# Folding Wv and Wo of six local-attention layers into one product per head, in a kernel on one core

## The chip, the core and the metric

The kernel runs on one core of a Trainium2 chip. The core has five engines, each with its own instruction stream: TensorE (PE; its weight loads are shown as PEld), VectorE (DVE), ScalarE (ACT), GpSimd (POOL) and SyncE (SP), which here only issues DMA copies. They synchronise by semaphores. Matmuls write to PSUM, eight banks of 512 fp32 columns by 128 partitions; the rest lives in SBUF. The metric is the device time of one execution in microseconds, as the median of several runs.

## The reference

x has 8 batch rows of 512 tokens by 128. An adaLN-modulated block applies a causal attention (16 heads of 8), then six local layers. One local layer is:

```python
def attn_layer(x, Wqkv, qs, ksc, Wo):        # Wqkv 128 x 3072, Wo 1024 x 128
    q, k, v = jnp.split(x @ Wqkv, 3, -1)     # 16 heads of 64
    q, k = l2norm(q) * qs, l2norm(k) * ksc   # per head
    ...                                      # rotary with scale on q and k
    out = local_attention(q, k, v)           # windows of 32, each sees itself and the one before
    return out.reshape(b, n, 1024) @ Wo
def ffn_layer(x, g, bln, W1, b1, W2, b2):    # layernorm, 128 -> 2 x 341, a * gelu(gate), -> 128
for i in range(6):
    x = attn_layer(shift_tokens(x), Wqkv[i], ...) + x
    x = ffn_layer(shift_tokens(x), ...) + x
```

`shift_tokens` takes the upper 64 dimensions from the token before. All is fp32.

## The kernel before

It has three parts, one after the other: the first attention (`modulated_attention`), the six local layers (`local_stack`), and a last residual.

**The local layers.** The work is cut into units, one batch row in one layer: 48 units, each of four tiles of 128 tokens. Each engine's program is a loop over units with the four tiles written out; the index d of a job says to which unit it belongs (0 this one, -1 the one before). The jobs of TensorE in one tile step stand in `jobs_of`, in the order in which TensorE runs them, each with its PSUM banks: the projections q, k and v (six fp32r matmuls each, of an input split in high and low parts), the transposes tq and tk of the tile before, ot (transposes of the attention's output o) of the tile three back, sim (the scores, 32 small products of 32 rows), pt (the transposes of the softmax weights), a feed job (m1 and m2 are the layernorm's mean and variance, y the second feed-forward product), z (Wo, eight products) and o (weights by values, 32 products), and in tile 1 the three hidden pieces h. `slot_free` makes TensorE wait until the earlier jobs in the same banks are taken out: so the table of banks decides which engine can hold up which job.

The other engines go through the same tiles in fixed orders. ScalarE squares q and k, copies qT, k_bd, v_tok, exponentiates the shifted scores in SBUF (`s`), copies oT and probT, makes the reciprocal norms by Ln and Exp, and does the layernorm's and gelu's functions. VectorE sums the squares, multiplies q and k by the cosine and sine tables (`rotate`), adds the mask, takes the maximum, sums the weights, divides o by the sum (L792), adds z and y to x. GpSimd adds the two halves of the rotation, applies the norms and subtracts the maximum.

The values go through SP: `spread_v` copies v_tok into v_bd, a layout with the windows of two heads side by side, block-diagonal with zeros, in eight copies a tile, and two more (the carried rows) from the tile before. v_tok and v_bd have two buffers, by the tile's parity. A value in `ready["o"]` two higher than the number of o jobs done lets SP fill a buffer once o of the tile two back is done. SP also loads the weights of the next layer (L337, in the last unit, before the last tile's spreading), the rotary tables, Wo and the feed-forward weights.

**The first attention** runs in 16 steps (heads) per batch row. Small jobs (`M_JOBS`: step, part, kind, distance in batches, group) use two banks in turn, so each waits for the one two places back. Beside it, one layer's Wqkv per batch row is split into high and low parts for the local layers: SP loads a third (L1052), GpSimd splits it (L1516, L1518), SP stores it (L1056).

## Time and profile before

| | |
|---|---|
| median of three runs | 3995.38 us (3992.62 to 4001.01) |
| the profiled execution | 4002.27 us, span 4000.5 us |
| mean granted TensorE clock | 0.985 |
| busy: PE / DVE / ACT / POOL | 93% / 79% / 64% / 70% |
| moved by DMA | 267.01 MB |

Times are in us from the start of the span unless marked ns. A clock of 1.00 is the upper of TensorE's two levels, 2.4 GHz. Matmuls overlap in the pipe and their ends are modelled, so how long one kind of job occupies TensorE is read from the start of the job to the start of the next. A wait shown in brackets is idle time just before an instruction, with the engine and line that ended it; "issue" means nothing that the profile shows.

### The profile page before, as it was taken

What the parts mean: (1) busy time and instruction counts of PE and PEld (TensorE: products, weight loads), DVE (VectorE), ACT (ScalarE), POOL (GpSimd) and SP (SyncE); (2) the same over time, 40 slices, a digit from 0 to 9 for tenths busy, and PEclk for the clock granted to TensorE, in tenths of its full rate; (3) what the DMA queues carried; (4) which work ended last, traced back from release to release, by engine and by line L of the source; (5) the groups of instructions that cost most, each with busy time, mean ns of one, the idle gap of its engine ahead of it and who ended that gap; (6) DMA issues with size and microseconds to landing.
All of it is one profiled execution on the core that took longest, in us unless ns stands there. A gap on an engine that the chain in (4) does not pass through costs nothing. (4 is left out here: it accounts for less than half of the span.)

```text
span 4000.5 us, 109740 instructions
## 1 busy us (share of the span) xinstructions
PE 3733.8 (93%) x42284; PEld 2927.6 (73%) x42284; DVE 3151.4 (79%) x4328; ACT 2570.7 (64%) x3589; POOL 2781.7 (70%) x2249
## 2 busy tenths in 40 slices
PE   6998897799999999999999999999999999999996
PEld 4766675677777777777777777777777777777774
DVE  4666664888888888888888888888888888888884
ACT  3555554566666666666666666666666767676763
POOL 2554552777777777777777777777777777777772
PEclk9999998999999999999999999999999999999998
DMA  1122110322223222232222232222322223222222
GB/s 42 59 74 73 66 68 13 100 66 60 62 63 100 66 58 64 55 103 63 68 53 66 82 79 64 61 61 62 102 66 62 60 60 99 62 70 54 68 54 62
DMA packets 157178, 267.01 MB, mean 67 GB/s; under 512 B 32062, under 2 KB 51644, under 8 KB 152380
## 3 DMA queue, kind: packets, MB, share of 16 engines
q1 hardware_dynamic: 157116, 266.19, 24.7%
q8 instruction: 38, 0.62, 0.1%
q14 instruction: 24, 0.20, 0.0%
HBM read 44.81 MB, written 26.21 MB: 18 GB/s over the span
## 5 line engine op out<-in xcount | busy, mean ns | idle before, releaser
L826 POOL TENSOR_TENSOR st_qk_rot<-st_qk_rot,st_qk_sq 128x1024 f32<-128x1024 f32 x384 | 920.5, 2402 | 692.7 <-DVE st_qk_sq L728 692.7
L455 PE MATMUL st_ps<-st_wqkv,st_xs 128*128 128x512 f32 x3456 | 949.6, 410 | 25.8 <-issue 18.3
L455 PEld LDWEIGHTS st_ps<-st_wqkv,st_xs 128*128 128x128 f32 x3456 | 608.2, 189 | 194.6 <-issue 75.2
L846 POOL TENSOR_TENSOR st_qk_rot<-st_qk_rot,st_rn 128x1024 f32<-128x1024 f32 x384 | 723.1, 1904 | 15.0
L710 DVE TENSOR_REDUCE st_nt<-st_qk_sq 128x16 f32<-128x1024 f32 x384 | 466.2, 1214 | 234.6 <-ACT st_qk_sq L573 233.2
L728 DVE TENSOR_TENSOR st_qk_sq<-st_ps,st_rot 128x512 f32<-128x512 f32 x768 | 490.1, 678 | 0.0
L714 DVE TENSOR_TENSOR st_qk_rot<-st_ps,st_rot 128x1024 f32<-128x1024 f32 x384 | 466.1, 1214 | 9.8 <-PE st_ps L472 9.8
L472 PE MATMUL st_ps<-consts_sb,st_qk_rot 128*128 128x128 f32 x3072 | 402.2, 274 | 27.9 <-DVE st_hid L802 14.9
L571 ACT ACTIVATE st_qk_sq<-st_ps 128x512 f32<-128x512 f32 x192 | 115.0, 599 | 486.3 <-PE st_ps L455 485.8
L472 PEld LDWEIGHTS st_ps<-consts_sb,st_qk_rot 128*128 128x128 f32 x3072 | 355.8, 141 | 94.1 <-DVE st_hid L802 34.7
L465 PEld LDWEIGHTS st_ps<-st_oT,st_wo 128*128 128x128 f32 x3072 | 368.8, 192 | 69.5 <-issue 67.7
L1458 DVE TENSOR_REDUCE at_nmx<-at_s 128x1 f32<-128x512 f32 (+3 forms) x512 | 236.9, 486 | 209.3 <-PE at_s L1103 208.5
L608 ACT ACTIVATE st_k_bd<-st_ps 64x1024 f32<-64x1024 f32 x384 | 389.5, 1014 | 3.1 <-PE st_ps L472 0.8
L485 PE MATMUL st_ps<-st_k_bd,st_qT 128*32 128x128 f32 x12288 | 375.2, 274 | 3.0 <-ACT st_k_bd L608 3.0
L465 PE MATMUL st_ps<-st_oT,st_wo 128*128 128x128 f32 x3072 | 376.2, 276 | 0.5 <-ACT st_oT L632 0.3
L497 PE MATMUL st_ps<-st_v_bd,st_probT 128*32 128x128 f32 x12288 | 375.2, 274 | 1.3 <-ACT st_probT L640 1.3
L874 POOL TENSOR_TENSOR st_s<-st_s,st_mx 128x1024 f32<-128x1024 f32 x192 | 366.0, 1906 | 6.1 <-DVE st_mx L753 6.1
L1279 ACT ACTIVATE at_probT<-at_t 128x512 f32<-128x512 f32 (+1 forms) x384 | 201.3, 526 | 255.8 <-PE at_t L1122 248.1
L485 PEld LDWEIGHTS st_ps<-st_k_bd,st_qT 128*32 128x32 f32 x12288 | 326.4, 110 | 35.6 <-ACT st_k_bd L608 20.5
L497 PEld LDWEIGHTS st_ps<-st_v_bd,st_probT 128*32 128x32 f32 x12288 | 323.7, 110 | 24.5 <-issue 1.5
L522 PE MATMUL st_ps<-st_xc,st_w 128*128 128x512 f32 (+1 forms) x576 | 261.8, 604 | 52.6 <-DVE xT_sb L784 43.2
L1542 POOL TENSOR_TENSOR at_qs<-at_q,consts_sb 128x512 fp32r<-128x512 f32 x128 | 135.3, 1074 | 216.8 <-DVE at_q L1409 200.0
(144 smaller groups left out, 6944.8 us busy)
## 6 DMA issues: line engine op xcount, KB each, us to landing
st_v_bd<-st_v_tok SPq DMA_DIRECT2D x1152, 128.0 KB, 2.4
st_v_bd<-st_v_tok SPq DMA_DIRECT2D x672, 64.0 KB, 2.1
wqkv_parts<-at_w_parts SPq DMA_DIRECT2D x18, 1024.0 KB, 4.6
st_wqkv<-wqkv_parts SPq DMA_DIRECT2D x18, 1024.0 KB, 7.0
at_w_raw<-in_wqkv SPq DMA_DIRECT2D x18, 512.0 KB, 5.1
rotary_tables<-at_rot SPq DMA_DIRECT2D x6, 512.0 KB, 3.4
st_rot<-rotary_tables SPq DMA_DIRECT2D x24, 128.0 KB, 2.4
st_wo<-in_wo SPq DMA_DIRECT2D x6, 512.0 KB, 4.4
```

The source lines that it names most:

```text
L455: last = pe.matmul(out[:, c * 512:(c + 1) * 512], xs[:, x_part, t * P:(t + 1) * P], rhs, start=(n == 0), stop=(n == len(PASSES) - 1))
L465: last = pe.matmul(out[:, 0:P], wo[:, c, :], oT[:, c * P:(c + 1) * P], start=(c == 0), stop=(c == IC - 1))
L472: last = pe.transpose(out[:, c * P:(c + 1) * P], src[:, c * P:(c + 1) * P], ident)
L485: last = pe.matmul(out[g * WIN:(g + 1) * WIN, c * P:(c + 1) * P], qT[:, par, c * P + g * WIN:c * P + (g + 1) * WIN], k_bd[:, c, :, key:key ...
L497: last = pe.matmul(out[g * WIN:(g + 1) * WIN, c * P:(c + 1) * P], probT[:, c * P + g * WIN:c * P + (g + 1) * WIN], v_bd[:, par, g, :, c * ...
L608: last = act.activation(k_bd[rows, :, a, WIN + t1 * P:WIN + (t1 + 1) * P], src[rows, :, :], ACT.Copy)
L710: dve.tensor_reduce(nt[:, 2 + par, heads], qk_sq[:, cols].rearrange("p (h d) -> p h d", d=DH), AX.X, ALU.add).then_inc(ss_sum, 1)
L714: dve.tensor_tensor(qk_rot[:, cols].rearrange("p (h d) -> p h d", d=DH), slot_of("qk"[a], 0, t).rearrange("p (h d) -> p h d", d=DH), rot[: ...
L728: last = dve.tensor_tensor(dst[:, :, g, :], src[:, :, 1 - g, :], sines.unsqueeze(1).to_broadcast([P, HEADS, DH // 2]), ALU.mult)
L826: pool.tensor_tensor(qk_rot[:, cols], qk_rot[:, cols], qk_sq[:, cols], ALU.add).then_inc(rot_done[a], 1)
L846: pool.tensor_tensor(view, view, rn[:, par, heads_of(a)].unsqueeze(2).to_broadcast([P, HEADS, DH]), ALU.mult).then_inc(normed[a], 1)
L874: pool.tensor_tensor(scores, scores, mx[:, tt % 2, :].unsqueeze(2).to_broadcast([P, HEADS, 2 * WIN]), ALU.subtract).then_inc(shifted, 1)
```

## The change

**Folding.** For each head, v times Wo's rows of that head equals x times (Wv Wo) of that head, a 128 by 128 matrix. The changed kernel makes these sixteen matrices once a layer, in the first attention: new small jobs transpose Wv's third of Wqkv (`vt`, two jobs of four transposes), multiply by Wo's rows (`fold`, four jobs of four products, a contraction of 64), ScalarE writes the high part, VectorE the low part, and SP stores 2048 columns, v0 (first heads of the pairs) and v1 (second heads). GpSimd splits only q and k.

**Projection.** The local layers project q, k, v0 and v1: four groups of six matmuls instead of three. A value row has 2048 columns instead of 1024.

**Products.** v_win has for each window 128 rows (two heads by 64 keys) and 128 columns per pair of heads. The 32 products of a tile now add up over the eight pairs into one 128-column bank, z. No zeros are needed, and the 8 transposes of o and the 8 products with Wo are gone. z (tokens first) is copied to SBUF (`z_tok`), transposed once (`zt`), and added to x.

**Softmax.** ScalarE exponentiates into PSUM banks 4 and 5 (`ex`), VectorE sums the weights there, and divides them there while writing them to `s`; pt transposes weights that are already divided, one tile later than before.

**Carried rows.** The last window of a tile is copied to `v_held` as soon as v is there, and from there into the next tile's windows. The spreading waits for z of the tile two back.

```diff
-H_BANKS = ((0, 1), (6, 7), (2, 3))
+H_BANKS = ((6, 7), (0, 1), (4, 5))
+PROJ = ("q", "k", "v0", "v1")
...
-            feed = {3: [(("m1", -1, 0), (1,))], 0: [(("m2", -2, 0), (1,))], 1: [], 2: [(("y", -2, 0), (1,))]}[t]
+            feed = {3: [(("m1", -1, 0), (6,))], 0: [(("m2", -2, 0), (6,))], 1: [], 2: [(("y", -2, 0), (6,))]}[t]
             hidden = [(("h", -2, j), H_BANKS[j]) for j in range(HC)] if t == 1 else []
-            return [tile("q", 0, 0, 1), tile("tq", 1, 2, 3), tile("k", 0, 4, 5), tile("tk", 1, 6, 7),
-                    tile("v", 0, 2, 3), tile("ot", 3, 0, 1), tile("sim", 1, 6, 7), tile("pt", 2, 2, 3), *feed,
-                    tile("z", 3, 0), tile("o", 2, 4, 5), *hidden]
+            return [tile("q", 0, 0, 1), tile("tq", 1, 2, 3), tile("k", 0, 4, 5), tile("ex", 2, 4, 5), tile("tk", 1, 6, 7),
+                    tile("v0", 0, 2, 3), tile("pt", 3, 0, 1), tile("sim", 1, 6, 7), tile("v1", 0, 0, 1), tile("z", 3, 2),
+                    *feed, *hidden, tile("zt", 3, 7)]
...
+                    for kind in ("v0", "v1"):
+                        sp.wait_ge(taken[kind], tiles_done(u, 0, t))
+                    if t < TILES - 1:
+                        d, carried = ((-1, 3), (-1, 2), (0, 1))[t]
+                        if alive(u, d):
+                            sp.sem_inc(filled, 1)
+                            sp.wait_ge(carry_in[carried % 2], carry_count(u, d, carried))
+                        for a in range(2):
+                            sp.dma_start(v_held[held_rows(t, a), :], v_tok[P - WIN:P, par, a, :]).then_inc(held_in[par], 16)
+                    sp.wait_ge(ready["z"], tiles_done(u, 0, t))
+                    if t:
+                        sp.sem_inc(filled, 1)
+                        sp.wait_ge(held_in[1 - par], held_count(u, 0, t - 1))
+                        for a in range(2):
+                            sp.dma_start(v_win[a * 2 * WIN:a * 2 * WIN + WIN, par, 0, :], v_held[held_rows(t - 1, a), :])\
+                              .then_inc(carry_in[par], 16)
                     for a in range(2):
                         rows = slice(a * 2 * WIN, (a + 1) * 2 * WIN)
-                        cols = slice(a * INNER // 2, (a + 1) * INNER // 2)
                         for g in range(1, WPT):
-                            sp.dma_start(v_bd[rows, par, g, a, :], v_tok[(g - 1) * WIN:(g + 1) * WIN, par, cols])\
-                              .then_inc(vbd_in[par], 16)
-                        sp.dma_start(v_bd[a * 2 * WIN + WIN:(a + 1) * 2 * WIN, par, 0, a, :], v_tok[0:WIN, par, cols])\
-                          .then_inc(vbd_in[par], 16)
+                            sp.dma_start(v_win[rows, par, g, :], v_tok[(g - 1) * WIN:(g + 1) * WIN, par, a, :])\
+                              .then_inc(win_in[par], 16)
+                        sp.dma_start(v_win[a * 2 * WIN + WIN:(a + 1) * 2 * WIN, par, 0, :], v_tok[0:WIN, par, a, :])\
+                          .then_inc(win_in[par], 16)
...
+                        if what == "wqkv" and t >= TILES - 2:
+                            for kind in (("q", "k"), ("v0", "v1"))[t - (TILES - 2)]:
+                                sp.wait_ge(ready[kind], tiles_done(u, 0, TILES - 1))
                                 load_wqkv(layer + 1, kind)
...
+                            elif kind == "zt":
+                                pe.wait_ge(taken["z"], tiles_done(u, d, index))
+                                last = pe.transpose(out[:, 0:P], z_tok[:, :], ident)
...
-                                            out[g * WIN:(g + 1) * WIN, c * P:(c + 1) * P],
+                                            out[g * WIN:(g + 1) * WIN, 0:P],
                                             probT[:, c * P + g * WIN:c * P + (g + 1) * WIN],
-                                            v_bd[:, par, g, :, c * DH:(c + 1) * DH], start=True, stop=True)
-                            elif kind == "ot":
-                                pe.wait_ge(taken["o"], tiles_done(u, d, index))
-                                for c in range(IC):
-                                    last = pe.transpose(out[:, c * P:(c + 1) * P], o[:, c * P:(c + 1) * P], ident)
+                                            v_win[:, par, g, c * P:(c + 1) * P], start=(c == 0), stop=(c == IC - 1))
...
+                        def copy_v(a):
+                            act.wait_ge(ready[f"v{a}"], n)
+                            if not (start and n < 3):
+                                act.wait_ge(win_in[t % 2], spread_count(u, d2, t2))
+                                if t2 < TILES - 1:
+                                    act.wait_ge(held_in[t2 % 2], held_count(u, d2, t2))
+                            act.activation(v_tok[:, t % 2, a, :], slot_of(f"v{a}", 0, t), ACT.Copy).then_inc(taken[f"v{a}"], 1)
...
+                            slot_free(act, u, STARTS[t] + EX_AT)
+                            act.activation(slot_of("ex", d2, t2), s[:, t2 % 2, :], ACT.Exp).then_inc(ready["ex"], 1)
...
+                            act.activation(z_tok[:, :], slot_of("z", d3, t3)[:, 0:P], ACT.Copy).then_inc(taken["z"], 1)
...
+                            dve.wait_ge(ready["ex"], n - 2)
+                            weights = slot_of("ex", d2, t2).rearrange("p (h k) -> p h k", h=HEADS)
+                            dve.tensor_reduce(den[:, t2 % 2, 0, :], weights, AX.X, ALU.add).then_inc(den_ready, 1)
                             dve.wait_ge(den_ready, 2 * (n - 2) - 1)
                             dve.reciprocal(den[:, t2 % 2, 1, :], den[:, t2 % 2, 0, :]).then_inc(den_ready, 1)
+                            dve.wait_ge(den_ready, 2 * (n - 2))
+                            dve.tensor_tensor(s[:, t2 % 2, :].rearrange("p (h k) -> p h k", h=HEADS), weights,
+                                              den[:, t2 % 2, 1, :].unsqueeze(2).to_broadcast([P, HEADS, 2 * WIN]),
+                                              ALU.mult).then_inc(taken["ex"], 1)
...
-SPLIT_STEPS = (2, 6, 14)
+SPLIT_STEPS = (5, 11)
...
-                  (7, 0, "round", -1, 3), (8, 0, "den", -1, 3), (8, 1, "mt", 0, 1), (9, 0, "rd", -1, 3),
+                  (7, 0, "round", -1, 3), (7, 1, "fold", 0, 0), (7, 1, "fold", 0, 1), (8, 0, "den", -1, 3), (8, 1, "mt", 0, 1), (9, 0, "rd", -1, 3),
...
+                def split_weights(layer):
+                    load_raw(layer, 2)
+                    sp.dma_start(wo_l[:, :, :], w["wo"][bass.ds(layer, 1), :, :].rearrange("l (c p) n -> p (l c) n", p=P))\
+                      .then_inc(fold_in, 16)
+                    sp.wait_ge(taken["vt"], layer * 2 + 4)
+                    sp.sem_inc(filled, 1)
+                    for a in range(2):
+                        load_raw(layer, a)
+                        sp.wait_ge(split_done, layer * 2 + (a + 1))
+                        store_parts(layer, a, w_parts[:, :, :])
+                def store_folded(layer):
+                    for a in range(2):
+                        sp.wait_ge(taken["fold"], layer * 4 + (2 * a + 6))
+                        store_parts(layer, 2 + a, fold_parts[:, a, :, :])
...
+                    elif kind == "vt":
+                        pe.wait_ge(raw_in, (b - 1) * 48 + 16)
+                        for i in range(TILES):
+                            at = (TILES * g + i) * P
+                            last = pe.transpose(out[:, i * P:(i + 1) * P], w_raw[:, at:at + P], ident)
+                    elif kind == "fold":
+                        rows, half = slice(g // 2 * DH, (g // 2 + 1) * DH), g % 2
+                        pe.wait_ge(taken["vt"], count(b, 0, 2, half))
+                        pe.wait_ge(fold_in, (b - 1) * 16 + 16)
+                        for i in range(TILES):
+                            c = TILES * half + i
+                            last = pe.matmul(out[:, i * P:(i + 1) * P], wvT[rows, c, :], wo_l[rows, c, :],
+                                             start=True, stop=True)
...
+                    elif kind == "vt":
+                        act.wait_ge(ready["vt"], count(b, d, 2, g))
+                        if g == 0:
+                            act.wait_ge(taken["fold"], count(b, -1, 4, 3))
+                        act.activation(wvT[:, TILES * g:TILES * (g + 1), :].rearrange("p c n -> p (c n)"), src[:, :], ACT.Copy)\
+                           .then_inc(taken["vt"], 1)
+                    elif kind == "fold":
+                        act.wait_ge(ready["fold"], count(b, d, 4, g))
+                        if g == 0:
+                            act.wait_ge(parts_out, (b - 1) * 64 + 16)
+                        act.activation(fold_parts[:, g // 2, 0, g % 2 * 512:g % 2 * 512 + 512], src[:, :], ACT.Copy)\
+                           .then_inc(fold_high, 1)
```

Three places in the order of instructions:

TensorE, one tile step before the unit's end, from the job after v on (st_o: attention output, st_s: weights, st_oT: its transpose), before:

```order
L505 MATMUL st_ps<-consts_sb,st_o 128x128 [waits st_o_taken,st_rot_read_q,st_squared_q]
L505 MATMUL st_ps<-consts_sb,st_o 128x128 x7
L485 MATMUL st_ps<-st_k_bd,st_qT 32x128 [waits st_tq_taken,st_tk_taken]
L485 MATMUL st_ps<-st_k_bd,st_qT 32x128 x31
L477 MATMUL st_ps<-consts_sb,st_s 128x128 [waits st_exp_ready,st_v_taken]
L477 MATMUL st_ps<-consts_sb,st_s 128x128 x7
L509 ISA [waits st_z_taken,st_ot_taken]
L509 MATMUL st_ps<-xT_sb,consts_sb 128x512
L465 MATMUL st_ps<-st_oT,st_wo 128x128 [waits st_wo_in,st_ot_taken]
L465 MATMUL st_ps<-st_oT,st_wo 128x128 x7
L494 REGISTER_ALU [waits st_pt_taken,st_vbd_in1,st_rot_read_k,st_squared_k]
L497 MATMUL st_ps<-st_v_bd,st_probT 32x128 [waits st_carry_in1]
```

and after, from the job after v0 on:

```order
L480 MATMUL st_ps<-consts_sb,st_s 128x128 [waits st_ex_taken,st_rot_read_q,st_squared_q]
L480 MATMUL st_ps<-consts_sb,st_s 128x128 x7
L488 MATMUL st_ps<-st_k_bd,st_qT 32x128 [waits st_tq_taken,st_tk_taken]
L488 MATMUL st_ps<-st_k_bd,st_qT 32x128 x31
L460 MATMUL st_ps<-st_wqkv,st_xs 128x512 [waits st_pt_taken]
L460 MATMUL st_ps<-st_wqkv,st_xs 128x512 x5
L495 REGISTER_ALU [waits st_pt_taken,st_v0_taken]
L500 MATMUL st_ps<-st_v_win,st_probT 32x128 [waits st_win_in0]
L500 MATMUL st_ps<-st_v_win,st_probT 32x128 x31
L507 ISA [waits st_zt_taken,st_sim_taken]
L507 MATMUL st_ps<-xT_sb,consts_sb 128x512
L469 MATMUL st_ps<-consts_sb,st_z_tok 128x128 [waits st_z_taken,st_sim_taken]
```

The transposes of o (L505) and the sixteen Wo instructions (L465) are gone; a projection (L460) stands between sim and the products, the products wait for v0 and the windows, and the mean product (L507) and one transpose (L469) come last.

VectorE, the last part of that tile, after the rotation, before:

```order
L749 TENSOR_TENSOR st_s<-st_ps,consts_sb 128x1024 [waits st_pt_ready,st_sim_ready]
L753 TENSOR_REDUCE st_mx<-st_s 128x16 [waits st_sim_taken]
L757 TENSOR_REDUCE st_den<-st_s 128x16 [waits st_exp_ready]
L760 RECIPROCAL st_den<-st_den 128x16 [waits st_den_ready]
L766 ISA [waits st_h_ready,st_m1_ready]
L766 TENSOR_TENSOR st_xc<-xT_sb,st_ps 128x512
L784 ISA [waits st_z_ready]
L784 TENSOR_TENSOR xT_sb<-st_ps,xT_sb 64x128
L784 ISA
L784 TENSOR_TENSOR xT_sb<-st_ps,xT_sb 64x128
L792 TENSOR_TENSOR st_o<-st_ps,st_den 128x1024 [waits st_ot_ready,st_den_ready,st_o_ready]
```

and after:

```order
L761 TENSOR_TENSOR st_s<-st_ps,consts_sb 128x1024 [waits st_pt_ready,st_sim_ready]
L768 TENSOR_REDUCE st_den<-st_ps 128x16 [waits st_ex_ready]
L770 RECIPROCAL st_den<-st_den 128x16 [waits st_den_ready]
L772 TENSOR_TENSOR st_s<-st_ps,st_den 128x1024 [waits st_den_ready]
L783 ISA [waits st_h_ready,st_m1_ready]
L783 TENSOR_TENSOR st_xc<-xT_sb,st_ps 128x512
L788 TENSOR_REDUCE st_mx<-st_s 128x16 [waits st_sim_taken]
L799 ISA [waits st_zt_ready]
L799 TENSOR_TENSOR xT_sb<-st_ps,xT_sb 64x128
L799 ISA
L799 TENSOR_TENSOR xT_sb<-st_ps,xT_sb 64x128
```

The division has moved from the end (o) to behind the reciprocal, where it works on the weights; the maximum has moved behind it and behind the layernorm's subtraction; z now waits for zt.

SP, in the last unit of a layer, around the loads of the next layer's weights, before:

```order
L360 ISA [waits st_rot_read_k]
L360 DMA st_rot<-rotary_tables 128x256
L397 REGISTER_ALU
L337 ISA [waits st_q_ready]
L337 DMA st_wqkv<-wqkv_parts 128x2048
L337 ISA [waits st_k_ready]
L337 DMA st_wqkv<-wqkv_parts 128x2048
L337 ISA [waits st_v_ready]
L337 DMA st_wqkv<-wqkv_parts 128x2048
L371 DMA st_v_bd<-st_v_tok 32x512 [waits st_o_ready,st_v_taken]
L371 DMA st_v_bd<-st_v_tok 32x512
L377 DMA st_v_bd<-st_v_tok 64x512 x3
```

and after, from the rows set aside for tile 2 on:

```order
L382 DMA st_v_held<-st_v_tok 32x1024
L387 REGISTER_ALU [waits st_z_ready]
L389 DMA st_v_win<-st_v_held 32x1024 [waits st_held_in1]
L389 DMA st_v_win<-st_v_held 32x1024
L394 DMA st_v_win<-st_v_tok 64x1024 x3
L396 DMA st_v_win<-st_v_tok 32x1024
L394 DMA st_v_win<-st_v_tok 64x1024 x3
L396 DMA st_v_win<-st_v_tok 32x1024
L367 ISA [waits st_rot_read_k]
L367 DMA st_rot<-rotary_tables 128x256
L349 ISA [waits st_v0_ready]
L349 DMA st_wqkv<-wqkv_parts 128x2048
```

Before, the three loads stood ahead of the last tile's copies. Now q's and k's stand ahead of the third tile's copies, v0's and v1's behind them, and those copies wait for z.

## Rows read from the trace of the kernel before

**Rows 1.** Windows by stage: length, busy per engine (count), PEclk, DMA share, GB/s.
```profile
300.00:450.00 150.00, 134.25 (x945) 103.00 (x935) 98.53 (x200) 86.20 (x167) 80.09 (x72) 0.98 0.22 77
2000.00:3000.00 1000.00, 971.03 (x11907) 770.24 (x11910) 843.72 (x1074) 685.02 (x897) 762.14 (x609) 1.00 0.27 70
```

**Rows 2.** st_wqkv's loads, then TensorE's timeline: start, us, what, count [idle before].
```profile
L337 SPq MOVE st_wqkv<-wqkv_parts x12: 29/29/38, 1755.8 to 3369.4; - x12
...
263.79 2.36 PE L1148 MATMUL at_m<-at_probT,at_v_pad 128*32 128x512 f32 x32
...
2007.06 1.06 PE L505 MATMUL st_ps<-consts_sb,st_o 128*128 128x128 f32 x8 [0.37 <-issue]
...
2017.34 1.66 PE L455 MATMUL st_ps<-st_wqkv,st_xs 128*128 128x512 f32 x6
2018.83 1.04 PE L472 MATMUL st_ps<-consts_sb,st_qk_rot 128*128 128x128 f32 x8
...
2023.37 1.04 PE L505 MATMUL st_ps<-consts_sb,st_o 128*128 128x128 f32 x8
2024.36 1.95 PE L485 MATMUL st_ps<-st_k_bd,st_qT 128*32 128x128 f32 x64
...
2028.33 1.95 PE L465 MATMUL st_ps<-st_oT,st_wo 128*128 128x128 f32 x16
2030.20 1.95 PE L497 MATMUL st_ps<-st_v_bd,st_probT 128*32 128x128 f32 x64
...
2061.92 5.41 PE L522 MATMUL st_ps<-st_xc,st_w 128*128 128x512 f32 x12 [0.94 <-DVE xT_sb L784]
...
2069.10 1.10 PE L472 MATMUL st_ps<-consts_sb,st_qk_rot 128*128 128x128 f32 x8 [0.33 <-DVE st_hid L802]
```

**Rows 3.** VectorE: waits of 800 to 3900; its timeline; the division's group.
```profile
DVE st_nt L710 <- ACT st_qk_sq L573: 227.5, 184, 1.7
DVE st_hid L802 <- ACT st_hid L670: 179.6, 93, 3.3
...
2034.79 1.22 DVE L710 TENSOR_REDUCE st_nt<-st_qk_sq 128x16 f32<-128x1024 f32 x1 [1.34 <-ACT st_qk_sq L573]
...
2041.96 0.41 DVE L686 TENSOR_TENSOR st_xs<-xT_sb,st_xs 128x256 fp32r<-128x256 f32 x1
...
L792 DVE TENSOR_TENSOR st_o<-st_ps,st_den 128x1024 f32<-128x1024 f32 x36 | 44.1, 1225 | 9.5 <-PE st_ps L497 8.6
```

**Rows 4.** ScalarE's timeline: rstd, the next square, the table after gelu.
```profile
2045.04 0.63 ACT L656 ACTIVATE st_rstd<-st_rstd 128x512 f32<-128x512 f32 x1
2048.13 0.60 ACT L571 ACTIVATE st_qk_sq<-st_ps 128x512 f32<-128x512 f32 x1 [2.46 <-PE st_ps L455]
...
2068.18 1.28 ACT L672 ACT_TABLE_LOAD   x1
```

**Rows 5.** SP's timeline of one burst; windows in bursts; st_wqkv's loads to landing.
```profile
2032.27 1.17 SPq L371 DMA_DIRECT2D st_v_bd<-st_v_tok  x2
...
2037.95 0.59 SPq L379 DMA_DIRECT2D st_v_bd<-st_v_tok  x1
...
2034.00:2036.00 2.00, 2.00 (x14) 1.68 (x13) 1.21 (x2) 1.53 (x2) 2.00 (x2) 1.00 0.71 164
1221.00:1223.00 2.00, 2.00 (x13) 1.52 (x13) 1.97 (x3) 1.18 (x2) 2.00 (x2) 1.00 1.02 430
...
DMA to landing us min/median/max: 4.9/7.0/10.2
```

**Rows 6.** TensorE's timeline at the start of the local layers.
```profile
722.95 1.94 PE L472 MATMUL st_ps<-consts_sb,st_qk_rot 128*128 128x128 f32 x8 [7.71 <-POOL st_qk_rot L846]
```

**Rows 7.** First attention: SP's stores of x1; the v job's group, 150 to 600.
```profile
400.01 0.33 SPq L1040 DMA_DIRECT2D x_dims_first<-at_x  x1
...
478.24 0.33 SPq L1040 DMA_DIRECT2D x_dims_first<-at_x  x1
...
L1173 PE MATMUL at_m<-at_wv,at_hT 128*128 128x128 f32 x42 | 6.2, 287 | 5.0 <-DVE at_aT L1428 5.0
```

266 lines of the change are left out of this document (124 added, 142 removed), and 3 rows, old and new, of the table M_JOBS.

## The prediction

> **What bounds the kernel now.** I read the windows by stage first, then TensorE's order of time over one unit, then the waits of VectorE, and last the copies. In the first attention TensorE is busy for 134 of 150 us. In the local layers it is busy for 971 of 1000 us, with VectorE at 844, ScalarE at 685, GpSimd at 762 and a granted clock of 1.00 [rows 1]. So TensorE sets the local stage, and VectorE is the engine behind it.
>
> The period of the local stage comes from the weight loads: from the group at 1755.8 to the last of the group three layers later, 3369.4, it is 1613.6 us less about 1 within a group, for 24 units (a unit is one batch row in one layer, four tiles): 67.2 us a unit [rows 2]. There are 48 units. In start-to-start times, a projection of six matmuls takes 1.49 (2017.34 to 2018.83), the eight transposes of o 0.99 (2023.37 to 2024.36), the sixteen instructions of Wo 1.87 (2028.33 to 2030.20). Three waits are seen in a unit: 0.37 before the transposes of o, 0.94 before the hidden layer, 0.33 before a query transpose [rows 2].
>
> VectorE's own work is 0.844 x 67.2 = 56.7 us a unit. It idles for ScalarE's squares (227.5 us over 184 tiles, 1.24 each) and for gelu (179.6 us over 46 units, 3.9 each) [rows 3]: it is ready early and waits for what TensorE feeds it.
>
> **Local layers, TensorE.** Removed per unit: 4 x (0.99 + 1.87) = 11.4 us, and the three waits, 1.64, since each hangs on a buffer that the new table of banks gives to another job or that is no longer made. Added: a fourth projection group, 4 x 1.49 = 5.96, and one transpose per tile, 4 x 0.15 = 0.6 (0.99 over eight, with something for the turn). The products with the weights stay 32 a tile with 128 columns; only where they add up changes. v_pad's products of the first attention already add up in strips of 32: 1280 columns in 2.36 us, 1.84 ns each, while o's 1024 take 1.95 us, 1.90 ns each [rows 2]. So I take no change (bounds 0 and +0.5 a tile). The work is then 67.2 - 11.4 - 1.6 + 6.0 + 0.6 = 60.8.
>
> New waits, found by setting the other engines' rows against that order:
> (a) The variance product now stands right before zt and the next q, with no z and o behind it (3.8 us). ScalarE makes rstd of it, until 2045.67 in the trace, and squares q at 2048.13 [rows 4]. With q 3.7 us sooner that square could start at 2044.4, so it comes about 1.2 late. VectorE starts late with it, and pt, whose banks are those of q, waits about 0.5.
> (b) After gelu ScalarE loads its table again, 1.28 [rows 4], so VectorE starts the next tile some 0.8 late: about 0.5 before pt.
> (c) VectorE has 7.2 us of rotation before the scores (2034.79 to 2041.96 [rows 3]), then mask, sum, division and maximum, some 1.2 each, and the reciprocal and z, 0.8 together: 12.8 us, in a tile for which TensorE needs 13.6: 60.8 less some 9.9 of small products (22 instructions like the twelve of the hidden layer, 5.41 [rows 2]) over four, and one small product. With the hidden layer it is 17.7. It fits with little to spare; I put 0.4 a unit for the places where it doesn't.
> Sum 1.4: a unit of 62.2, 5.0 less. These rates hold from about 745, when the pipeline has filled, to 3915: 3170 / 67.2 = 47 units, **-235 us**.
>
> VectorE's and ScalarE's work stays: the division reads the same 1024 columns from PSUM as the one over o did (1225 ns [rows 3]), the copy of v1 takes the place of oT's, z_tok adds an eighth of such a copy and its start, some 0.3 a tile. The sum over weights moves its source from SBUF to PSUM. A reduction of 1024 from SBUF takes 1.22 us and the product from PSUM 1225 ns [rows 3]: I take 0, bounds -0.05 and +0.1 a tile. By the Trainium skill (VectorE: DVE Perf Modes, the section on the TRN2 errata) an instruction with a source in PSUM has a fixed cost 62 cycles above one with a source in SBUF, some 65 ns. That would be 12 us of VectorE over 192 tiles, inside its spare time. The rows show no such difference at this size.
>
> **The copies.** Each tile issues ten copies for its windows as before, and two more for the rows set aside. Ten issues take 6.3 us (2032.27 to 2038.54 [rows 5]). A row of a copy has 4 KB instead of 2 KB, so a burst has 2.1 MB instead of 1.05. With 2 KB rows a burst used 0.71 of the queues at 164 GB/s, which is 230 at full share; with 8 KB rows the weights moved 430 GB/s at 1.02 [rows 5]. In time per row this is 142 and 305 ns on each of 16 queues, and between them some 196 ns at 4 KB: 330 GB/s, or 6.4 us a burst, as long as its issue. A weight load of 1.05 MB lands 4.9 us after its issue at the least [rows 5], of which 2.4 is transfer, so the last copy lands about 6.3 + 2.5 + 0.2 = 9.0 after z. The new waits hang on this: v_tok of a tile is written again in the tile after next, but its windows are only free after z of the tile two back, which comes one tile later than o did. From the end of z to ScalarE's copy of v0 there are at least 1 us of small products, then q, tq, k, tk, v0, pt and the copy of probT: about 9.3 us in the tightest tile. It just fits: 0, bounds 0 and +1 us in two tiles of a unit.
>
> **Layer boundaries.** SP is in order. The loads of v0 and v1 now stand behind the third tile's windows, which wait for the z of the tile two back; before, all three loads went out ahead of the last tile's windows. From the end of that z: ten issues 6.3, a table 0.6, then v0's load, which lands 4.9 later [rows 5]: 11.8. TensorE wants v0 after m1 0.9, zt 0.15, and q, tq, k, tk, which took 4.54 (2017.34 to 2023.37, less v's 1.49 [rows 2]): 5.6. It stands for 6.2 us. After 7.71 us of standing, eight transposes took 1.94 instead of 1.04 [rows 6], and I allow the same once more for what follows: 8 us at each of five boundaries, **+40** (bounds 0 and 60).
>
> **First attention.** Batches follow each other at 78.2 us (400.01 to 478.24 [rows 7]). Six of them get two jobs of four transposes (0.5 each) and four folding jobs, each four products like the v job (6.2 us over 5.25 jobs and some overlap [rows 7]: 0.95): 4.8 us of TensorE. They share two banks with all small jobs, each job waits for the one two back, and a folding job is released only after ScalarE's copy and VectorE's subtraction a step later. I add 1.5 a batch: 6.3 x 6 = **+38** (bounds: 14, if half the work sinks into the 8 us a batch in which TensorE waits now [rows 1], and 65, if each of the six jobs makes a wait of 1). GpSimd loses a third of the splitting, which nobody waits for.
>
> At the start a fourth load stands before the small ones: +2.4, less a little for the shorter clearing, **+2**. The tail I leave as it is.
>
> Sum: -235 + 40 + 38 + 2 = -155 on the profiled execution's 4002.3: 3847. The median of the runs is 3995.4, 0.2% lower, so **3840**.
>
> **Rivals.**
> *VectorE takes over.* It has 56.7 us of work a unit, and its idle time may hang on the order and not on TensorE's pace. If the 1.24 per tile before the squares stays, and a third of gelu's 3.9, it is 63.0, and 64 with delays that push each other: 3.2 x 47 = 150 gained, 80 paid, 3925. For it: 12.8 in 13.6 is little room, and z of the tile now comes last on both engines. Against: the banks let VectorE lag. 0.2.
> *The additions are free.* The loads come in time, and the folding sinks into present waits: -235 + 14 + 2, 3775. SP's order speaks against it. 0.1.
> *The windows' copies set the pace: slower.* If a burst moves no more than the 164 GB/s seen, 2.1 MB takes 12.8 us and lands 15.1 after z; the copy of v0 (1.0) and z (1.9), whose bank was v0's, close the loop: 18.0 a tile, 72 a unit, 4.8 x 47 + 80 = +306, 4300. It decides for slower from 65.5 a unit on, a landing 13.5 after z. Against it: the share was 0.71, not 1. The Trainium skill (DMA: Bandwidth & Descriptors, "Why small descriptors are slow") says that copies within SBUF don't pay for small rows, and that the fabric limits them at 435 GB/s. The 230 at full share with 2 KB rows does not agree with that, the 430 with 8 KB rows does; by it a burst would take 4.8 us. 0.05.
> *Adding up in one bank costs what the fold saves*, 1.2 us a tile: about 3995. v_pad's row speaks against it. 0.03.
>
> **Numbers.** The forecast has 0.62: 3840. The range is 3765 to 3925, from free additions to VectorE's case. Against the 0.2% that a measurement tells from no change: faster 0.92, the same 0.03, slower 0.05.
>
> **What the profile will show.** A unit of 62 us with TensorE near 60 and VectorE over 90%; no wait before the hidden layer, short ones before pt; bursts of ten copies in 6 us, the last landing 9 us after z; five gaps of 6 us before v0; batches of 84 us in the first attention; some 510 MB moved. I am wrong if a unit takes over 64, if ScalarE's copy of v0 waits for copies in each tile, or if batches grow by more than 11 us.

## The result, and the profile after

| | before | after |
|---|---|---|
| median, us (4 runs each, side by side) | 3997.92 (3992.62 to 4001.01) | 4059.08 (4052.26 to 4062.88) |
| ratio | 1 | 1.0152, 95% interval 1.0133 to 1.0172 |
| span of the profiled execution | 4000.5 | 4059.3 |
| loads for the local layers issued at | 696.8 | 746.3 |
| period of a unit | 67.2 | 65.7 |
| a unit across a layer boundary, less that | 0 | 13.1 (10.5 to 16.4) |
| moved by DMA | 267.01 MB | 512.39 MB |

The change makes the kernel 1.5% slower; the forecast was 3840. A unit's period is read from one first gelu to the next. After, in ScalarE's timeline (start, us, engine, line; an idle time before in brackets):

```profile
2055.63 1.26 ACT L679 ACTIVATE st_hid<-st_ps,st_b 128x512 f32<-128x512 f32 x2
...
2121.32 1.26 ACT L679 ACTIVATE st_hid<-st_ps,st_b 128x512 f32<-128x512 f32 x2
```

65.7 us, where 62.2 was forecast. TensorE no longer fills the stage, and no other engine does; the window that answers to [rows 1]:

```profile
2000.00:3000.00 1000.00, 911.49 (x10899) 674.31 (x10899) 855.77 (x1069) 683.37 (x949) 765.35 (x608) 0.98 0.65 142
```

The waits of 900 to 3900 (engine, tile, line, releaser: us, times, longest) say what stands between them:

```profile
ACT st_v_tok L598 <- DMA st_v_win<-st_v_tok: 227.3, 129, 3.0
...
DVE st_den L768 <- ACT st_ps L633: 145.3, 129, 2.1
...
PE st_ps L480 <- issue: 92.3, 173, 1.0
...
PE st_ps L500 <- ACT st_v_tok L598: 79.9, 85, 1.7
...
PE st_ps L460 <- DMA st_wqkv<-wqkv_parts: 56.3, 8, 11.1
```

ScalarE's copy of v0 waits for the window copies in 129 tiles: three of the four of a unit. Behind it stand its own exponential, for which VectorE waits as often (129 times), and z, whose bank is v0's. The loop can be followed in one tile. TensorE, then SP's queue, then ScalarE:

```profile
2034.47 1.95 PE L500 MATMUL st_ps<-st_v_win,st_probT 128*32 128x128 f32 x64 [0.95 <-ACT st_v_tok L598]
...
2044.62 1.06 PE L480 MATMUL st_ps<-consts_sb,st_s 128*128 128x128 f32 x8 [0.95 <-issue]
...
2050.08 1.95 PE L500 MATMUL st_ps<-st_v_win,st_probT 128*32 128x128 f32 x64 [0.93 <-ACT st_v_tok L598]
```

```profile
2036.69 1.17 SPq L389 DMA_DIRECT2D st_v_win<-st_v_held  x2
...
2040.97 2.60 SPq L394 DMA_DIRECT2D st_v_win<-st_v_tok  x3
2043.61 0.99 SPq L396 DMA_DIRECT2D st_v_win<-st_v_tok  x1
```

```profile
2048.92 1.02 ACT L598 ACTIVATE st_v_tok<-st_ps 128x1024 f32<-128x1024 f32 x1 [2.18 <-DMA st_v_win<-st_v_tok]
```

z ends at 2036.4, the ten copies are issued from 2036.69 to 2044.6 (8 us, not 6.3), the last has landed at 2048.9, 12.5 after z; then the copy of v0, and the next z at 2050.08: 15.6 us round. The next round has the hidden layer in it and lasts to 2069.13, 19.1 us; there the loop has time. Over the whole stage the medians from one z to the next are 15.4, 15.6, 19.1 and 15.7 us. The queues are full in such a burst (the share is the last but one number, GB/s the last); over the four windows of 2008 to 2016 the rate is 197 to 260, on average 221:

```profile
2008.00:2010.00 2.00, 2.00 (x14) 1.70 (x12) 1.94 (x5) 0.94 (x2) 2.00 (x2) 1.00 1.04 197
```

At a layer boundary TensorE stands for v0's weights. SP's queue, and TensorE:

```profile
1279.63 0.94 SPq L349 DMA_DIRECT2D st_wqkv<-wqkv_parts  x2
```

```profile
1289.30 2.90 PE L460 MATMUL st_ps<-st_wqkv,st_xs 128*128 128x512 f32 x6 [11.01 <-DMA st_wqkv<-wqkv_parts]
```

The load is issued behind ten window copies and a table and its data arrive 9.7 us later, behind theirs. From this projection's start to the next job's (1292.00) it is then 2.70 us instead of 1.49 [rows 2], at the lower clock level (granted 0.50 from 1289 to 1293). At three of the five boundaries TensorE had also waited for k's weights, 1.1 to 3.5 us. In the first attention, between the stores of x1 (78.2 us before [rows 7]) lie 89.6 us:

```profile
430.04 0.33 SPq L1060 DMA_DIRECT2D x_dims_first<-at_x  x1
519.61 0.33 SPq L1060 DMA_DIRECT2D x_dims_first<-at_x  x1
```

From the traces alone: 49.5 us in the first attention (746.3 against 696.8), 66 at the five boundaries, 5 in filling the pipeline (to the first gelu), 5 in the last two periods, less 1.47 (67.18 against 65.71) for each of the other 45 periods, 66. Sum about +59; the spans differ by 58.8.

### The profile page after: what moved, and what is told of

It reads as the page before. It is cut to its first block and busy times, and to the rows that moved or that the text cites. A ratio compares the mean times of both kernels' runs of the same rounds, so it can differ in the third digit from the quotient of the medians.

```text
span 4059.3 us, 104487 instructions
## 1 busy us (share of the span) xinstructions
PE 3598.6 (89%) x39260; PEld 2658.4 (65%) x39260; DVE 3208.4 (79%) x4352; ACT 2604.8 (64%) x3817; POOL 2756.6 (68%) x2238
## 2 busy tenths in 40 slices
DMA packets 172730, 512.39 MB, mean 126 GB/s; under 512 B 36862, under 2 KB 56444, under 8 KB 166396
## 5 line engine op out<-in xcount | busy, mean ns | idle before, releaser
L460 PE MATMUL st_ps<-st_wqkv,st_xs 128*128 128x512 f32 x4608 | 1273.3, 412 | 99.7 <-DMA st_wqkv<-wqkv_parts 56.3
L460 PEld LDWEIGHTS st_ps<-st_wqkv,st_xs 128*128 128x128 f32 x4608 | 815.7, 190 | 336.9 <-issue 194.0
L598 ACT ACTIVATE st_v_tok<-st_ps 128x1024 f32<-128x1024 f32 x384 | 389.9, 1015 | 248.5 <-DMA st_v_win<-st_v_tok 244.2
L500 PE MATMUL st_ps<-st_v_win,st_probT 128*32 128x128 f32 x12288 | 376.1, 274 | 90.1 <-ACT st_v_tok L598 86.7
L500 PEld LDWEIGHTS st_ps<-st_v_win,st_probT 128*32 128x32 f32 x12288 | 325.1, 110 | 165.0 <-issue 155.9
L883 POOL TENSOR_TENSOR st_s<-st_s,st_mx 128x1024 f32<-128x1024 f32 x192 | 374.3, 1949 | 48.7 <-DVE st_mx L788 48.7
L768 DVE TENSOR_REDUCE st_den<-st_ps 128x16 f32<-128x1024 f32 x192 | 235.0, 1224 | 162.6 <-ACT st_ps L633 160.5
L625 ACT ACTIVATE st_probT<-st_ps 128x1024 f32<-128x1024 f32 x192 | 196.9, 1025 | 231.2 <-PE st_ps L480 231.2
L480 PE MATMUL st_ps<-consts_sb,st_s 128*128 128x128 f32 x1536 | 208.9, 280 | 98.9 <-issue 97.7
```

The costliest lines, as they stand in the source:

```text
L460: last = pe.matmul(out[:, c * 512:(c + 1) * 512], xs[:, x_part, t * P:(t + 1) * P], wqkv[:, PROJ.index(kind), w_part, c * 512:(c + 1) * 51 ...
L500: last = pe.matmul(out[g * WIN:(g + 1) * WIN, 0:P], probT[:, c * P + g * WIN:c * P + (g + 1) * WIN], v_win[:, par, g, c * P:(c + 1) * P], ...
L598: act.activation(v_tok[:, t % 2, a, :], slot_of(f"v{a}", 0, t), ACT.Copy).then_inc(taken[f"v{a}"], 1)
L883: pool.tensor_tensor(scores, scores, mx[:, tt % 2, :].unsqueeze(2).to_broadcast([P, HEADS, 2 * WIN]), ALU.subtract).then_inc(shifted, 1)
```

## Experiments

Each kernel is the changed one with the edit shown; of an edit only the lines that matter stand here, some of them shortened, and the counts of the semaphores follow. Ratios are to the kernel before, run beside it, with 95% intervals; after it stands at 1.0152.

### 1. v0's copy waits for its own half of the windows only

```diff
-act.wait_ge(win_in[t % 2], spread_count(u, d2, t2))
+act.wait_ge(win_in[t % 2][a], spread_count(u, d2, t2))
```

Each half's copies have a semaphore of their own, and z waits for both.

> ScalarE's copy of v0 waits only for the window copies that read v0's half of v_tok (the first five of a burst's rows of it), and that of v1 for the others; the number and size of copies stay. Theory A (the handoff of v_tok through the window copies sets three of the four tiles of a unit: z, burst of 8.0 us, last landing 4.6 later, copy of v0 1.0, next z): v0's copy is released four issues earlier, 3.7 us, its waits of 1.1 to 2.2 us go, and a unit falls from 65.7 to 62.2 to 63.0 us; 45 units give -120 to -155 us: 3905 to 3940, ratio to the kernel before 0.977 to 0.986. Theory B (the waits for copies only show what another chain, ScalarE and VectorE around the exponential in PSUM, would take anyway): a unit stays within 0.7 of 65.7 and the time at 4030 to 4060, ratio 1.008 to 1.015. The five gaps at the layer boundaries stay in both.

Measured: 3958.47, ratio 0.9907 (0.9891 to 0.9924). A unit takes 63.6 us. ScalarE's wait for window copies is gone; the boundaries cost 12 to 17 as before, now 13.4. Nothing was made faster, the wait only leaves out the four window copies of the other half: theory A holds for 2.1 of the 3.5 us. It leaves 1.4 open, and the time came out 18 us above its range. The rounds from z to z are now 14.0, 15.1, 18.9 and 15.7 us (medians). So of the three waits of v0's copy two cost TensorE time, 1.4 and 0.5 us; the third, in the round of 15.7, which has the second feed-forward product in it, cost nothing.

### 2. All weight loads ahead of the third tile's burst

```diff
-if what == "wqkv" and t >= TILES - 2:
-    for kind in (("q", "k"), ("v0", "v1"))[t - (TILES - 2)]:
+if what == "wqkv" and t == TILES - 2:
+    for kind in PROJ:
```

> All four weight loads of the next layer are issued ahead of the third tile's burst; nothing else. Theory A: the wait for v0's weights of 9 to 11 us per boundary goes, but 4.2 MB now stand in front of one burst and hold the windows up, so some 5 us a boundary stay of the 13.5 that a boundary costs: 5 x 8.5 = -42 us, 4017, ratio 1.005 (1.001 to 1.009). Rival: the stall only moves to the windows behind the loads and the time stays at 4059, ratio 1.015.

Measured: 4033.09, ratio 1.0093 (1.0072 to 1.0114). A boundary costs 8.7 us instead of 13.1. TensorE no longer waits for weights there, but one tile later for z, since v0's copy waits for windows that are queued behind 4.2 MB. ScalarE and TensorE of this kernel:

```profile
1280.93 1.02 ACT L598 ACTIVATE st_v_tok<-st_ps 128x1024 f32<-128x1024 f32 x1 [9.26 <-DMA st_v_win<-st_v_tok]
```

```profile
1282.18 3.64 PE L500 MATMUL st_ps<-st_v_win,st_probT 128*32 128x128 f32 x64 [8.19 <-ACT st_v_tok L598]
```

### 3 and 4. No folding jobs; only the transposes of Wv

```diff
-(2, 1, "vt", 0, 0), (3, 1, "vt", 0, 1),
...
-(7, 1, "fold", 0, 0), (7, 1, "fold", 0, 1), (11, 1, "fold", 0, 2), (14, 1, "fold", 0, 3),
...
+store_parts(layer, 2 + a, w_parts[:, :, :])
```

> The first attention makes no folded weights: the six vt and fold jobs of a batch row are left out, Wv's third is loaded but not used, and the parts of q and k are stored a second time in the places of v0 and v1, so that SP moves the same bytes; the local layers do the same work on other numbers. If the jobs themselves (work and the waits of two banks) cost the 49.5 us by which the local layers start later than before: they start at 697 to 702 and the time falls by 45 to 50 us, to 4010 to 4015, ratio 1.003 to 1.005. Rival: a part of it comes from the splitting that moved to later steps and from SP's order: less than 30 us come back, ratio above 1.008.

> Of the folding jobs in the first attention only the two that transpose Wv's third stay; the four folding jobs of a batch row are left out, and q's and k's parts are stored in the places of v0 and v1. Leaving out all six gave back 54.7 us on the changed kernel's 4059.1. If a job's cost goes by its work on TensorE (two of four transposes 0.4 to 0.5 each, four of four products 1.1 each): the four are 44 to 50 of the 54.7, so 4010 to 4015, ratio 1.003 to 1.005. If each of the six costs alike through the two banks: 36 of it, 4023, ratio 1.0065.

Measured: 4004.41, ratio 1.0020 (1.0011 to 1.0030), and with vt 3999.79, ratio 1.0006 (0.9996 to 1.0015). The local layers' loads go out at 696.2 and at 690.9 (746.3 in the changed kernel). (The second run keeps the two vt jobs.) So leaving out the four folding jobs brings the loads 55 us forward, 9 a batch row (the total falls by 59), and leaving out the transposes too gives nothing more: more than either theory gave the four. The first run, without any of the six, has its loads 5 us later than the second; why is open. That in the second they go out 6 us before those of the kernel before (696.8) may come from GpSimd's shorter splitting, but the first run has that as well, and it was not tried alone.

### 5. Half the bytes

```diff
-sp.dma_start(v_win[rows, par, g, :], v_tok[(g - 1) * WIN:(g + 1) * WIN, par, a, :])
+sp.dma_start(v_win[rows, par, g, 0:512], v_tok[(g - 1) * WIN:(g + 1) * WIN, par, a, 0:512])
```

> Each window copy, the carried ones too, moves only the first 512 of its 1024 columns (2 KB rows, as in the kernel before), and the products read these twice: twelve copies a tile as in the changed kernel, half the bytes. Theory A: a burst is issued in 6.3 us and lands 2.4 us after its last issue, as before, so 8.9 after z instead of 12.4, and no copy of v0 waits: a unit of 62.2 to 62.8, the boundaries a little better, 3895 to 3930, ratio 0.974 to 0.983. Theory B: a unit stays at 65 to 65.7, ratio 1.008 to 1.015.

Measured: 3929.63, ratio 0.9831 (0.9815 to 0.9848). As many copies, half the bytes: SP's issue is back to 6.3 us, a copy lands after 2.4 us instead of 4.6, no copy of v0 waits, a unit takes 63.6 as in the first run, with the same four rounds, a boundary costs 8.0. It is the bytes that hold the handoff up, and 63.6 is the next limit.

### 6 and 7. Windows from DRAM, in copies of 64 and of 128 partitions

```diff
-sp.dma_start(v_win[rows, par, g, :], v_tok[(g - 1) * WIN:(g + 1) * WIN, par, a, :])
+sp.dma_start(v_win[rows, par, g, :], w_split[par, (g - 1) * WIN:(g + 1) * WIN, a * INNER:(a + 1) * INNER])
```

and in the second run, once for both halves:

```diff
+sp.dma_start(v_win[:, par, g, :], w_split[par, :, (g - 1) * 512:(g - 1) * 512 + INNER])
```

> The changed kernel with one thing else: the eight window copies of a tile, with the same 4 KB rows, the same destination and the same waits, read DRAM (the weights' scratch) and not v_tok, so the products use other numbers. It tells what made a burst of 2.1 MB take 9 us and more. Theory R (the length of the rows: a 4 KB row takes what it takes, near 300 ns a queue): the landing stays at 12.4 after z, a unit at 65 to 66, ratio 1.011 to 1.017. Theory S (the source in SBUF: the weights came from DRAM at 430 GB/s, copies within SBUF at some 225): a burst moves at over 350 GB/s, lands within 9.5 us after z, no copy of v0 waits, a unit of 63.6 as in the runs that released it, 3925 to 3960, ratio 0.982 to 0.991.

> As the run with the windows read from DRAM (4150 us, its bursts at 205 to 240 GB/s at full share), but each of the three whole windows of a tile comes in one copy of 128 partitions instead of two of 64; rows of 4 KB and bytes are the same. Theory P (what sets the rate is how many partitions a copy spans: 64 reach half of the SBUF's DMA ports, 128 all, as for the weights): the middle of a burst moves over 350 GB/s, the landing comes some 4 us earlier, a unit falls from 67.6 to 63.6 to 64.5, 3940 to 4000, ratio 0.986 to 1.001. Theory R (a 4 KB row costs 300 ns wherever it goes, and 8 KB rows cost no more): the rate stays near 215 GB/s and a unit at 66 or above, ratio above 1.02.

Measured: 4150.39, ratio 1.0390 (1.0373 to 1.0407), and 3942.43, ratio 0.9858 (0.9842 to 0.9874). Of the first run's two theories the one on the source fell: from DRAM a copy lands later (5.5 us against 4.6), the burst moves no faster, and v0's copy starts 13.2 us after z against 12.5. Theory R's range (a unit of 65 to 66) was missed as well: a unit takes 67.7. R still seemed nearer, until the second run, with rows of the same 4 KB, came to twice the rate in the middle of a burst, at full share. (It has five copies for eight, but the queues are full in both.) Its unit is 63.6; v0's copy starts 2.5 us earlier than with 64 partitions, where 4 were expected. The run with 64 partitions, then that with 128:

```profile
2016.00:2018.00 2.00, 1.92 (x10) 1.61 (x11) 1.99 (x4) 1.97 (x3) 1.05 (x2) 1.00 1.07 225
```

```profile
2004.00:2005.00 1.00, 1.00 (x5) 0.83 (x5) 1.00 (x2) 0.98 (x2) 1.00 (x1) 1.00 1.05 422
...
2024.00:2025.00 1.00, 1.00 (x7) 0.82 (x6) 1.00 (x2) 1.00 (x2) 0.00 (x0) 1.00 0.98 401
```

What sets the rate is how many partitions a copy spans: from DRAM 64 get 203 to 231 GB/s in the windows of a burst at full share, 128 get 401 and 422 in the middle of a burst, as the weights did [rows 5]. The Trainium skill says so (SBUF — State Buffer, "Door 1: The DMA port swizzle"): partitions 0 to 63 reach eight of the SBUF's sixteen DMA ports, for some 218 GB/s, all 128 reach sixteen, for 436. Both levels agree with these runs; the ports themselves no trace shows.

The traces' records of single packets have the same step. A packet of 4 KB took 320 ns (median of a burst) to 64 partitions, from SBUF as from DRAM, and 159 in the middle of a burst to 128. To 64 partitions one of 2 KB took 142 ns, to 128 one of 8 KB 309. So the length of the rows has little part in it here. Copies within SBUF that span 128 partitions were not tried.

### 8. The two halves in turn

```diff
-for a in range(2):
-    for g in range(1, WPT):
+for g in range(1, WPT):
+    for a in range(2):
```

> The changed kernel with the six copies of whole windows issued window by window, first heads' 64 partitions and then second heads', in turn, where they were issued all first heads' and then all second heads'. Bytes, rows and waits are the same. If copies to the two halves of the partitions overlap in the queues (theory P with some depth): full-share rate of 300 GB/s or more, landing 2 to 3 us earlier, a unit of 63.6, 3950 to 3965, ratio 0.989 to 0.992. If one copy after the other goes through all queues in step: 65.7 a unit, 4059, ratio 1.015.

Measured: 3992.43, ratio 0.9987 (0.9977 to 0.9996), from the order of issue alone. A unit takes 64.5, a boundary costs 10.7; the wait of v0's copy falls from 227.3 us to 167.0. It lies between the two expectations: two halves in turn overlap a little. Three of the kernel's windows:

```profile
2024.00:2025.00 1.00, 1.00 (x4) 0.20 (x2) 0.75 (x2) 0.60 (x2) 1.00 (x2) 1.00 1.04 320
2025.00:2026.00 1.00, 0.66 (x3) 0.36 (x3) 1.00 (x3) 0.52 (x1) 1.00 (x1) 1.00 1.01 234
2026.00:2027.00 1.00, 1.00 (x5) 0.82 (x5) 1.00 (x2) 0.98 (x2) 0.97 (x2) 1.00 1.08 246
```

The Trainium skill (SBUF — State Buffer, "Can I just issue two DMAs to hit both halves?") says no, with a gain of 6%. The size agrees: over nine such windows (2021 to 2030) the mean is 230 GB/s, against 221 over the four of 2008 to 2016 in the changed kernel. But the path hung on it: v0's copy starts 11.6 to 11.9 us after z where it was 12.2 to 12.5, and so 4% on each burst gave 1.6% of the kernel's time.

### 9. What holds a unit at 63.6

```diff
-dve.tensor_reduce(mx[:, t1 % 2, :], scores, AX.X, ALU.max)
+dve.tensor_reduce(mx[:, t1 % 2, :], scores[:, :, WIN:WIN + 8], AX.X, ALU.max)
```

Edit 1 is in it too.

> v0's copy waits only for its own half of the window copies, and VectorE takes the maximum over 8 of the 64 keys of a head (0.3 us for 1.2), 0.9 us less in each tile, which leaves most scores out of the maximum. It tells what holds a unit at 63.6 once the copies don't. If VectorE (890 of 1000 us busy there): a unit falls by 1 to 1.5 to 62.1 to 62.6, TensorE's own pace by the forecast, 3890 to 3912, ratio 0.973 to 0.979. If TensorE's work is simply longer than forecast: a unit stays at 63.6 and the ratio at 0.991.

Measured: 3922.6, ratio 0.9813 (0.9797 to 0.9830); a unit of 62.9. The four maxima of a unit take 276 ns instead of 1210: 3.7 us a unit taken from VectorE give 0.7. It is neither of the two cases, and the time is 11 us above the range of the first.

With edit 1 TensorE still waits 2.6 us in a unit: 0.95, 0.40 and 0.48 before pt, 0.34 before q's projection (for VectorE's product in the feed-forward layer) and 0.41 before a transpose (for GpSimd). Each of the three pt starts 0.1 us after VectorE's second read of q's bank ends. In the run with edit 1, VectorE, then TensorE:

```profile
2017.02 1.28 DVE L738 TENSOR_TENSOR st_qk_sq<-st_ps,st_rot 128x512 f32<-128x512 f32 x2
```

```profile
2018.40 1.06 PE L480 MATMUL st_ps<-consts_sb,st_s 128*128 128x128 f32 x8 [0.40 <-issue]
```

The wait of 0.95 comes where VectorE is busy without a break, and the lighter VectorE cuts it to 0.29. Those of 0.40 and 0.48 stay (0.41 and 0.46): there VectorE had stood idle for 0.66 and 0.32 before q's sum, in the run with edit 1 already, so its amount of work is not what they hang on. In both runs the period less the waits (2.6 and 1.9) is 61.0: TensorE's work, forecast at 60.8.

### 10 to 12. Edits together

> The two edits of the first runs together: v0's copy waits only for its own half of the window copies, and all four weight loads stand ahead of the third tile's burst. If the two costs are separate, the gains add up: 101 and 26 us, 3932, ratio 0.984 (0.981 to 0.987). With them the boundary's price is 8 us, since v0's own windows still stand behind 4.2 MB of weights. Rival: the earlier loads meet a burst that is now tighter and give back nothing: 3958, ratio 0.991.

> v0's copy waits only for its own half of the window copies; q's, k's and v0's loads stand ahead of the third tile's burst, v1's between its two halves. v0's windows then wait for 3.1 MB that had been asked for from 11 us before z on, so they land on time, and v1's load lands some 12 us after z where TensorE wants it 10 after: a boundary costs 3 us and not 13: -50 on the run with the halves alone, 3908, ratio 0.978 (0.975 to 0.982). Rival: the loads are slower than 430 GB/s beside the rows set aside and the tables, and it ends where all four early do, at 3932, 0.984.

> Alternating window copies, v0's copy waiting only for its own half of them, and all weight loads ahead of the third tile's burst. If alternating overlaps the copies: the boundary gets shorter too, 3895 to 3910, ratio 0.975 to 0.979. If it doesn't: v0's half now lands one issue before the end instead of four, its wait returns in part, a unit of 64.5 to 65.5: 3960 to 4000, ratio 0.991 to 1.001.

Edits 1 and 2: 3916.29, ratio 0.9796 (0.9780 to 0.9813). Faster than their sum: a boundary costs 5.7 us on average. With edit 1 and v1's load between the halves of the burst (`for kind in PROJ[:3]`, then `load_wqkv(next_layer, "v1")` after the first half): 3925.46, ratio 0.9819 (0.9803 to 0.9836), 8.7 a boundary, so against all four loads early the idea gave nothing, and neither its 3908 nor its rival's 3932 came. Edits 1, 2 and 8: 3940.84, ratio 0.9860 (0.9838 to 0.9881), between the two ranges: a unit of 63.6, but 9.7 a boundary. Alternating puts v0's last window one issue before the end, and behind the weights that counts. The wait of v0's copy did return, in two tiles of a unit (91 times from 900 to 3900), but outside the boundaries it cost nothing: the unit stays at 63.6.

### 13 and 14. The folded bank freed by ScalarE

```diff
-act.activation(fold_parts[:, g // 2, 0, g % 2 * 512:g % 2 * 512 + 512], src[:, :], ACT.Copy).then_inc(fold_high, 1)
+act.activation(fold_raw[:, g // 2, cols], src[:, :], ACT.Copy).then_inc(taken["fold"], 1)
+act.wait_ge(taken["fold"], count(b, d, 4, g))
+act.activation(fold_parts[:, g // 2, 0, cols], fold_raw[:, g // 2, cols], ACT.Copy).then_inc(fold_high, 1)
...
-dve.tensor_tensor(fold_parts[:, g // 2, 1, at:at + 512], src[:, :],
-                  fold_parts[:, g // 2, 0, at:at + 512].bitcast(F32), ALU.subtract).then_inc(taken["fold"], 1)
+pool.tensor_tensor(fold_parts[:, a, 1, :], fold_raw[:, a, :], fold_parts[:, a, 0, :].bitcast(F32),
+                   ALU.subtract).then_inc(fold_low, 1)
```

> The changed kernel with one thing else, in the first attention: ScalarE copies the folded product as it is to SBUF, which frees the bank at once, and makes the high part from there; the low part is made by GpSimd from SBUF in two instructions a batch row, and VectorE's four subtractions out of PSUM (0.68 us each) go. If the bank, held until VectorE's turn, is what the folding costs beyond its products: 2.5 to 4.5 us a batch row come back, 4033 to 4045, ratio 1.009 to 1.012. If not, or if GpSimd's two long instructions (2.4 us each) hold up its picks of q: no gain or a loss, 4055 to 4075, ratio 1.0145 to 1.019.

> The best version so far (v0's copy waits for its own half of the window copies, all weight loads ahead of the third tile's burst: 0.9796) with the low parts of the folded weights made by GpSimd. The stages follow each other, so it should differ from 3916 by what the same edit does to the changed kernel alone: -15 to -25 us if the bank is what costs, 3891 to 3901, ratio 0.973 to 0.976; 3916 or above if not.

Measured: 4057.03, ratio 1.0155 (1.0138 to 1.0172), and 3927.92, ratio 0.9825 (0.9809 to 0.9841). No gain in either, and the second is 12 us above edits 1 and 2 alone: that VectorE holds the bank is not what the folding costs, or GpSimd's part takes it back. These runs don't tell which.

## Why the prediction was wrong

The forecast was faster, with a chance of 0.92; the kernel came out slower, which had 0.05.

**The copies: the step that failed.** The prediction said "between them some 196 ns at 4 KB: 330 GB/s", a landing 9.0 after z, and so no wait, bounds 0 to 1 us in two tiles. I read two rates, 230 GB/s at full share with 2 KB rows and 430 with 8 KB rows [rows 5], as a matter of row length and put 4 KB between them. The two kinds of copy differ in another way as well: 64 partitions against 128. Runs 6 and 7 show that this is what counts. With the 230 of the rows the sum would have been 2.1 MB in 9.1 us, and 2.5 + 0.2 behind it: 11.8 after z (12.5 measured) against 9.3 available (9.8 in the tightest tile of run 5, where no copy of v0 waits). The third rival named the loop rightly: z, burst, copy of v0, z. It had the mechanism and a wrong price, 72 a unit where 65.7 came, for two reasons. It took 164 GB/s without dividing by the share. And it asked for a loop of over 16.4 us in each of four tiles before the change would be slower, but a tile that has time lends none to the others: with rounds of 15.4, 15.6, 19.1 and 15.7 the landing of 12.5, below its threshold of 13.5, was enough. The rival was given 0.05. The loop's price in the total, from runs 1 and 5: 2.1 us a unit, some 95 us.

**The work of TensorE** (60.8 a unit) was right: 61.0. Products that add up in one bank cost what they did. **The new waits** were given 1.4; with the copies out of the way they are 2.6 (run 9). The wait named in (a) is 0.95 instead of 0.5, that in (b) 0.40 instead of 0.5, the rest before pt 0.48 where (c) has 0.4; 0.34 before q's projection and 0.41 for GpSimd were not in the sum. So the first rival was right in the number, 63.6 where it had 63, but in its cause for 0.7 us at most: that is what a lighter VectorE gives. VectorE's sum and division from PSUM take 1.22 to 1.23 where [rows 3] have 1225 ns, against 1.21 for the maximum from SBUF; the 0 that was put there holds. The tile with the hidden layer comes to 18.1 by the terms of (c), 12.7 and 5.4, not 17.7; nothing hangs on it.

**Boundaries**: forecast 8 each, measured 13.1. The order of SP was read rightly (the load behind ten issues and a table), but a load was given the 4.9 us of an undisturbed one; behind 2.1 MB at 215 GB/s it needs 9.7. The waits for k's weights were not in it either. Run 5, with half the bytes, has 8.0.

**First attention**: forecast 38, measured 49.5. The jobs' cost is in the four folding jobs alone (runs 3 and 4), 9 us a batch row where 3.8 of work and some 1 of waiting were put. In the trace after, the products take 5 us of TensorE's busy time a batch row, not 3.8, and TensorE waits 1.8 for the subtraction. Run 13 says that taking that subtraction away changes nothing in sum. Where the rest of the 9 us arises stays open; jobs at other steps were not tried.

**The sum.** Against the forecast, in us: the copies some 95, what is left of the unit 1.4 x 45 = 63 (1.2 of waits, 0.2 of work), the boundaries 26, the first attention 11, the filling 3: 198 of the 214 between 3847 and 4061. Of the rest some 10 come from the forecast's 47 units at 5.0, where only 45 periods are steady, and 5 from the last two, which are longer than before.

The signs that the prediction named worked: a unit over 64 and v0's copy waiting for copies in each tile (three of four) were both there, and "batches grow by more than 11 us" in one of five: the batches take 85 to 91 us where they took 78 to 82, and grow by 6.4 to 11.3.

The change is sound in what it does to TensorE. With two edits to waits and order that cost nothing it gives 3916, 2% less than before (0.9796), though every byte of its 512 MB is still moved.

## What to carry to other kernels

A rate read from a busy queue is worth more than an interpolation between two kinds of copy: first list all in which they differ, the number of partitions above all. Where a handoff between engines goes through copies, count the loop from the release of the buffer to its next use against the period of each tile by itself, not against the mean of a unit, and let each user wait only for the copies that read its own part. A wait that a profile shows has a price only where the next engine stands for it: here two of three had one. A queue that is in order makes each load that stands behind a burst as late as the burst's bytes, not as its issues.

## What the hardware showed that I had not expected

- Copies to 64 partitions: on average 221 GB/s from SBUF, 203 to 231 from DRAM, at a full share of the queues; the same rows of 4 KB from DRAM to 128 partitions: 401 to 422. A packet of 4 KB took 320 ns in the one case and 159 in the other.
- Three issues on SP took 2.60 us instead of 1.88 (1.87 in run 5) while the queues were full.
- Taking the two halves of the partitions in turn raised the rate of a burst by only 4% (221 to 230) and cut the kernel's time by 1.6%.
- From DRAM, the copies of 64 partitions landed 5.5 us after their issue, within SBUF 4.6 (medians); measured from z the difference in run 6 is 0.7 us, and its issues were shorter (0.58 to 0.60 us each against 0.61 to 1.02).
